# Cell work of each expert moved by a gate unit, a second place for the forget gate, and halves stored in pairs, in a language-model tower on one core

## The chip, the core and the metric

One NeuronCore of a Trainium2 chip runs the whole program as one launch. The metric is device time in microseconds, from the first to the last instruction and what the launch adds around it, as the median of three executions.

## What is computed

16 sequences of 512 tokens go through one block. Tokens become 128 features: an embedding and a projected spectrum per frame. Then h = h + attention(layernorm(h)), with 8 heads of 16, 64 summary tokens of full attention and a window of 17 for the other 448. Then comes the part that takes most of the time, a mixture of 8 recurrent experts, of which each token is given 2:

```python
logits = flat_x @ router_w + router_b
top_vals, top_idx = jax.lax.top_k(logits, K)          # K = 2 of E = 8
rw = jax.nn.softmax(top_vals, axis=1)
mask = (top_idx.T[:, None, :] == jnp.arange(E)[None, :, None])
expert_x = (mask[..., None] * flat_x[None, None]).reshape(K, E, S_, B_, I_)
def step(carry, xt):                                   # scanned over the 16 sequences
    h, c = carry
    i_, f_, g_, o_ = jnp.split(xt @ Wi + h @ Wh + b, 4, axis=-1)
    c = sigmoid(f_) * c + sigmoid(i_) * tanh(g_)
    h = sigmoid(o_) * tanh(c)
    return ((h, c), h @ Wo + bo)
y = jnp.einsum('ken,nk,keno->no', mask, rw, out)
```

Every expert sees every token of both choices, masked to zero where it was not chosen, since its state runs on.

## The kernel before

**Steps and units.** A step of the recurrence is one sequence. It has 32 gate units t = 4e + g: expert e = 0 to 7, and within it the gates I, G, F, O (g = 0 to 3). Each engine has a loop over s and t, written out by hand, and works through its list in order; nothing is planned by a scheduler. Beside the units of step s every engine runs `front(t, s + 1)`, the piece of embedding, attention and routing of the next sequence that the tables `PE_AT`, `ACT_AT`, `DVE_AT` and `SP_AT` (lines 56 to 63) give to unit t. Unit t of TensorE, ScalarE and VectorE are the same t, each after what the engine waits for.

**A gate.** TensorE (`unit_gate`, line 486) makes a gate of both choices, 128 x 1024, in 12 matmuls of 512 columns (line 506): weights and moving data are split into a high and a low 16-bit half, and three of the four products are taken, for input and state. There are two gate banks, so gate n waits for the tanh of gate n-2. ScalarE (`gate_tanh`, line 644) takes the tanh into a place of `tmp` (sigmoids are tanhs of half the argument).

**The cell on VectorE**, per expert, each operation on 128 x 1024: `input_part` (line 1000, writes (1+I)G), `cell` (line 1010: (1+F)C, line 1013, then C, line 1017), ScalarE's `cell_tanh` (line 658), which writes into F's only place, `hidden` (line 987: h in O's place), ScalarE's `split_hi` (line 664: high half of h), `hidden_lo` (line 995: low half), and `chosen` (line 1020): a predicated copy takes h of the choice that the token made, a product with its weight (line 1032) goes to `z32`. TensorE multiplies that by Wo (`unit_y`, line 509) into one bank; after all experts `y_out`, `y_back` and `add_y` bring it to the output. `masked_input` (line 975) makes the masked input of the next expert.

**Order on VectorE before** (lines 1044 to 1067). g=0: hidden(e-1), front. g=1: masked_input(e+1), hidden_lo(e-1), front, input_part(e). g=2: chosen(e-1), front, cell(e). g=3: front. In unit 30 masked_input of the next step's expert 0 comes first.

**SyncE** has the queue of DMA issues, in order too (lines 359 to 373). In units g=1 it loads masks for expert e+2 (`mask_in`, line 330). In units g=3 it loads the two row broadcasts of expert e+1 (`rows_in`, line 341), after waiting for the product of chosen(e-1):

```python
                if n >= 2:
                    sp.wait_ge(s_z, n - 1)
```

In unit 28 it stores the next step's masks and weights to DRAM (`SP_AT["rows"]`, line 312); in units 29 and 30 it broadcasts the masks of experts 0 and 1 back, after both stores have landed; in unit 31 come the rows of expert 0, and in unit 0 the next token ids (`sp_ids`, line 319), which line 779 turns into a one-hot and line 420 into the embedding.

**The routing** ends on VectorE with the front of unit 26 (line 973, the router weights); TensorE transposes them in unit 27 (line 483), and ScalarE evicts them (lines 639 and 642).

**Attention's block-diagonal weights.** `diag` holds, for 28 blocks of 16 queries, the heads of q and later the windows of v in a block-diagonal form, as two planes of 16-bit halves. It is filled by four DMAs from `pr` (SyncE, unit 6, line 310) and again from `vwin` (ScalarE's queue, unit 9, line 619) and read as 128-column weights, 84 times by line 447 and 84 times by line 459. The windows of v are made by two transposes, one a plane (line 824).

## Time and profile before

| | us |
|---|---|
| median of three executions | 1915.93 (1915.46 to 1918.11) |
| the profiled execution | 1918.11 |
| its span | 1916.3 |
| TensorE busy, matmul | 1729.1 (90%) |
| VectorE busy | 1559.5 (81%) |
| ScalarE busy | 991.9 (52%) |
| first gate matmul | at 120.2 |
| span of one steady step | about 114 |

Busy is the time in which an engine had an instruction under way, as a share of the span. Matmuls overlap in the pipeline and their ends are modelled, so TensorE's share is not a share of its peak. The granted clock of TensorE is 0.97 of full over the span, 1.00 in most of the steady part. A number in brackets behind a timeline row is the idle time of the engine before it, with what ended it. All times of views are from the start of the span.

### The profile page before, as it was taken

The page shows a single profiled execution, that of the slowest core. Times are in us where ns is not written, and L with a number is a line of the kernel's source. Part 1 is how long each engine was busy: PE and PEld are TensorE (multiplying, and loading weights), DVE is VectorE, ACT ScalarE, POOL GpSimd, SP SyncE. Part 2 cuts the span into 40 slices and gives each one's busy share as a digit, 9 for nine tenths or more (in the row PEclk, how much of TensorE's full clock was granted, in tenths as well). Part 3 has the DMA queues.
Part 4 walks back from the last instruction along what each step waited for, and adds up shares of the span by engine and source line. Part 5 has one row for each costly group of instructions (what it writes and reads, how often), then busy time and mean ns, then how long its engine had stood idle before and what let it go on. Part 6 is the DMA issues. An engine that isn't in the chain of part 4 may idle for free.

```text
span 1916.3 us, 25885 instructions
## 1 busy us (share of the span) xinstructions
PE 1729.1 (90%) x9898; PEld 837.6 (44%) x9898; DVE 1559.5 (81%) x2433; ACT 991.9 (52%) x1114; POOL 65.2 (3%) x42
## 2 busy tenths in 40 slices
PE   3457799999999999999999999999999999999998
PEld 2223344444444444444444444444444444444443
DVE  2649698897988889798898988889898888979865
ACT  3234554646555555645545455455555555564544
POOL 1000000000000000000000000000000000000000
PEclk9668899999999999999999999999999999999999
DMA  3113241413314132232313224151331413223221
GB/s 114 20 41 74 57 67 46 77 37 67 63 49 74 39 70 52 52 70 51 67 45 69 51 57 67 44 80 37 63 66 46 76 37 71 53 50 67 55 61 36
DMA packets 318594, 110.95 MB, mean 58 GB/s; under 512 B 240331, under 2 KB 299581, under 8 KB 318471
## 3 DMA queue, kind: packets, MB, share of 16 engines
q1 hardware_dynamic: 202758, 101.96, 23.9%
q10 hardware_dynamic: 115712, 7.34, 3.8%
q8 instruction: 78, 1.28, 0.3%
q14 instruction: 46, 0.37, 0.1%
HBM read 89.84 MB, written 4.74 MB: 49 GB/s over the span
## 4 chain that ended last, share of the span: by engine, by line
PE 40%; DVE 33%; DMA 8%; issue 7%; ACT 5%; ACTq 4%; SPq 1%; POOL 0%; DVEq 0%
PE gates L506 25%; ACTq L619 4%; DVE C L1017 4%; DVE tmp L1007 4%; DMA masks<-mask_scratch 3%; DVE tmp L1013 3%; DMA prod<-in_x_ids 3%; DVE xm L985 3%; PE yp L512 3%; DVE Hs L997 3%; DVE tmp L1028 3%; DVE xn L795 2%; PE FA L447 2%; ACT tmp L655 2%; PE FA L459 2%
## 5 line engine op out<-in xcount | busy, mean ns | idle before, releaser
L655 ACT ACTIVATE tmp<-gates,bias_sb 128x1024 f32<-128x1024 f32 x504 | 557.5, 1109 | 558.6 <-PE gates L506 496.1
L506 PE MATMUL gates<-xm,wi_sb 128*128 128x512 f16 x3024 | 747.3, 384 | 46.2 <-ACT tmp L655 31.0
L506 PE MATMUL gates<-Hs,wh_sb 128*128 128x512 f16 x2880 | 704.4, 381 | 0.0
L506 PEld LDWEIGHTS gates<-xm,wi_sb 128*128 128x128 f16 x3024 | 290.3, 99 | 435.3 <-issue 105.1
L506 PEld LDWEIGHTS gates<-Hs,wh_sb 128*128 128x128 f16 x2880 | 283.2, 98 | 344.3 <-issue 8.0
L662 ACT ACTIVATE tmp<-C 128x1024 f32<-128x1024 f32 x128 | 135.2, 1057 | 226.4 <-DVE C L1017 223.2
L992 DVE SCALAR_TENSOR_TENSOR tmp<-tmp 128x1024 f32<-128x1024 f32 x128 | 155.9, 1218 | 71.8 <-ACT tmp L662 71.8
L1007 DVE SCALAR_TENSOR_TENSOR tmp<-tmp 128x1024 f32<-128x1024 f32 x120 | 144.9, 1208 | 46.4 <-ACT tmp L655 44.9
L985 DVE TENSOR_TENSOR xm<-xs,masks 128x2048 f16<-128x2048 f16 x128 | 155.2, 1212 | 32.7 <-DMA masks<-mask_scratch 32.7
L997 DVE SCALAR_TENSOR_TENSOR Hs<-tmp,Hs 128x1024 f16<-128x1024 f32 x120 | 146.4, 1220 | 37.7 <-ACT Hs L666 36.7
L1013 DVE SCALAR_TENSOR_TENSOR tmp<-tmp,C 128x1024 f32<-128x1024 f32 x120 | 146.4, 1220 | 14.4 <-ACT tmp L655 14.0
L1017 DVE SCALAR_TENSOR_TENSOR C<-tmp 128x1024 f32<-128x1024 f32 x120 | 147.0, 1225 | 4.1
L666 ACT ACTIVATE Hs<-tmp 128x1024 f16<-128x1024 f32 x120 | 126.5, 1055 | 31.2 <-DVE tmp L992 30.7
L512 PE MATMUL yp<-z,wo_sb 128*128 128x512 f32 x256 | 134.9, 609 | 8.2 <-DVE z L1032 8.2
L1105 POOL TENSOR_TENSOR rstd<-veps,mhalf 128x4 f32<-128x4 f32 x32 | 61.6, 1926 | 1682.6 <-DVE veps L922 1114.8
L1032 DVE TENSOR_TENSOR z<-tmp,roww 128x512 f32<-128x512 f32 x128 | 88.6, 692 | 13.6 <-DVE tmp L1028 0.5
L1028 DVE COPY_PREDICATED tmp<-rowk,tmp 128x512 f32<-128x512 uint16 x128 | 93.0, 727 | 0.1
L512 PEld LDWEIGHTS yp<-z,wo_sb 128*128 128x128 f32 x256 | 48.0, 194 | 38.8 <-issue 12.2
L459 PE MATMUL FA<-vwin,diag 128*128 128x32 f16 x1344 | 36.3, 177 | 7.4 <-DVE vwin L882 7.4
L447 PEld LDWEIGHTS FA<-xn,diag 128*128 128x128 f16 x1344 | 38.2, 97 | 8.1 <-issue 5.5
L459 PEld LDWEIGHTS FA<-vwin,diag 128*128 128x128 f16 x1344 | 36.0, 96 | 12.5 <-DVE vwin L882 9.2
L447 PE MATMUL FA<-xn,diag 128*128 128x32 f16 x1344 | 39.1, 178 | 0.0
(155 smaller groups left out, 1218.9 us busy)
## 6 DMA issues: line engine op xcount, KB each, us to landing
masks<-mask_scratch SPq DMA_DIRECT2D x128, 256.0 KB, 5.0
roww<-mw_scratch SPq DMA_DIRECT2D x128, 256.0 KB, 4.0
rowk<-mask_scratch SPq DMA_DIRECT2D x128, 128.0 KB, 3.0
diag<-pr SPq DMA_DIRECT2D x64, 112.0 KB, 4.3
diag<-vwin ACTq DMA_DIRECT2D x64, 112.0 KB, 4.8
out_dram<-h SPq DMA_DIRECT2D x16, 256.0 KB, 3.7
C<-in_wi SPq DMA_DIRECT2D x1, 2048.0 KB, 10.9
C<-in_wh SPq DMA_DIRECT2D x1, 2048.0 KB, 15.6
```

Source lines behind the costliest of these rows:

```text
L506: last = mm(gates[:, slot, k * SEQ:(k + 1) * SEQ], w, v, start=(i < K), stop=(i >= len(seq) - K))
L512: mm(yp[:, :], wo_sb[:, e, :], z32[:, :], start=False, stop=(e == E - 1)).then_inc(s_y, 1)
L655: A(tmp[:, gate_at(gate, e), :], gates[:, (n - 1) % 2, :], ACT.Tanh, bias=bias_sb[:, e, gate:gate + 1], scale=UNSCALE).then_inc(s_tanh, 1)
L662: A(tmp[:, TANH_C, :], C[:, e, :], ACT.Tanh, scale=0.5).then_inc(s_tc, 1)
L666: A(Hs[:, e, HI, :], tmp[:, gate_at(O, e), :], ACT.Copy, scale=V_SCALE).then_inc(s_hhi, 1)
L985: TT(xm[:, e % 2, :, :, :], xv, mv_, ALU.mult).then_inc(s_xm, 1)
L992: STT(out=at, in0=at, scalar=1.0, in1=tmp[:, TANH_C, :], op0=ALU.add, op1=ALU.mult).then_inc(s_h, 1)
L997: STT(out=Hs[:, e, LO, :], in0=tmp[:, gate_at(O, e), :], scalar=V_SCALE, in1=Hs[:, e, HI, :], op0=ALU.mult, op1=ALU.subtract).then_inc(s_h ...
L1007: STT(out=at_i, in0=at_i, scalar=1.0, in1=at_g, op0=ALU.add, op1=ALU.mult).then_inc(s_u, 1)
L1013: STT(out=at_f, in0=at_f, scalar=1.0, in1=C[:, e, :], op0=ALU.add, op1=ALU.mult).then_inc(s_v, 1)
L1017: STT(out=C[:, e, :], in0=at_f, scalar=0.5, in1=tmp[:, gate_at(I, e), :], op0=ALU.mult, op1=ALU.add).then_inc(s_c, 1)
L1028: V.copy_predicated(at[:, 0:SEQ], rowk1[:, e % 2, :].bitcast(u16), at[:, SEQ:2 * SEQ]).then_inc(s_sel, 1)
```

## The change

The cell of expert e moves behind its O gate: VectorE's order becomes g=0: cell(e-1), front; g=1: masked_input(e+1), front, hidden(e-1); g=2: front, input_part(e); g=3: hidden_lo(e-1), chosen(e-1), front. ScalarE takes the cell tanh after the next expert's I tanh and the high half in g=2. TensorE's y matmuls and the bias of y move from g=0 to g=1, SyncE's store from unit 9 to 10. `tmp` has eight places: F has two, and the cell tanh goes to its own expert's F place. The weighted state stays in the upper half of O's place, so `z32` and the wait on it go, and O's tanh waits for the y matmul of two experts back. In `qz`, the v halves, `vwin` and `diag` the two 16-bit halves of a number lie side by side, so that one 32-bit transpose and 32-bit DMA elements carry both, and the matmuls of lines 447 and 459 read their weights at a stride of two. The waits and order of `rows_in`, `mask_in` and the stores on SyncE are as before.

```diff
@@ -85,14 +85,13 @@
         Hs = sb("Hs", [P, E, 2, K * SEQ], f16)
-        tmp = sb("tmp", [P, 7, K * SEQ])
+        tmp = sb("tmp", [P, 8, K * SEQ])
...
         roww = sb("roww", [P, 2, SEQ])
-        z32 = sb("z32", [P, SEQ])
@@ -116,7 +115,7 @@
         oW = sb("oW", [P, NW])
-        diag = sb("diag", [P, 2, NBLK, NG, 2 * DH], f16)
+        diag = sb("diag", [P, NBLK, NG, 2 * DH])
@@ -131,12 +130,13 @@
         wT = rows[WT0:WT0 + E, :]
-        qz = pr[:, :].bitcast(f16).rearrange("p (v j c q) -> p v j c q", v=2, j=NBLK, c=2)
+        qz = pr[:, :].bitcast(f16).rearrange("p (j c q v) -> p j c q v", j=NBLK, c=2, v=2)
...
         pr16, prT16 = pair16(pr[:, :], NBLK * KB), pair16(prT[:, :], NBLK * KB)
-        vw16 = vwin[:, :].bitcast(f16).rearrange("p (v j d) -> p v j d", v=2, j=NBLK)
-        vhl = ew[:, 0:TF + 2 * PAD].bitcast(f16).rearrange("p (v t) -> p v t", v=2)
+        vwj = vwin[:, :].rearrange("p (j d) -> p j d", j=NBLK)
+        vp = ew[:, 0:TF + 2 * PAD]
+        vp16 = pair16(vp, TF + 2 * PAD)
@@ -170,15 +170,18 @@
         def gate_at(gate, e):
 
-            return {I: e % 2, G: 2 + e % 2, F: 4, O: 5 + e % 2}[gate]
-
-        TANH_C = gate_at(F, 0)
+            return {I: 0, G: 2, F: 4, O: 6}[gate] + e % 2
+
+        def chosen_at(e):
+
+            return tmp[:, gate_at(O, e), SEQ:2 * SEQ]
...
         fid = tmp[0:NFFT, 2, 512:512 + NBJ].bitcast(i32)
-        diag_flat = diag[:, :, :, :, :].rearrange("p v j g d -> p (v j g d)")
-        onehot64 = diag_flat[0:NFFT, 2 * VOCAB * NBJ:3 * VOCAB * NBJ]
-        mag = diag_flat.bitcast(f32)[0:NFREQ, 0:VOCAB * NBJ]
+        diag_flat = diag[:, :, :, :].rearrange("p j g d -> p (j g d)")
+        diag16 = diag_flat.bitcast(f16).rearrange("p (j m v) -> p j m v", j=NBLK, v=2)
+        onehot64 = diag_flat.bitcast(f16)[0:NFFT, 2 * VOCAB * NBJ:3 * VOCAB * NBJ]
+        mag = diag_flat[0:NFREQ, 0:VOCAB * NBJ]
@@ -307,8 +310,8 @@
                     for g in range(NG):
-                        load(diag[32 * g:32 * g + 32, :, :, g, :].rearrange("p v j d -> p (v j) d"),
-                             qz[32 * g:32 * g + 32, :, :, :, :].rearrange("p v j c q -> p (v j) (c q)"), S["qbd"])
+                        load(diag[32 * g:32 * g + 32, :, g, :],
+                             pr[32 * g:32 * g + 32, :].rearrange("p (j d) -> p j d", j=NBLK), S["qbd"])
@@ -359,7 +362,7 @@
             def step(s, par, first, last):
...
                     e, g = t // NG, t % NG
-                    if t == 9 and not first:
+                    if t == 10 and not first:
@@ -444,7 +447,7 @@
                             for qv, kv in ((HI, HI), (HI, LO), (LO, HI)):
-                                last = mm(FA[:, r, jj * KB:(jj + 1) * KB], diag[:, qv, j, :, :].rearrange("p g d -> p (g d)"),
+                                last = mm(FA[:, r, jj * KB:(jj + 1) * KB], diag16[:, j, :, qv],
@@ -456,7 +459,7 @@
                         for vv, pv in ((HI, HI), (HI, LO), (LO, HI)):
-                            last = mm(FA[:, j // HB, (j % HB) * KB:(j % HB + 1) * KB], diag[:, vv, j, :, :].rearrange("p g d -> p (g d)"),
+                            last = mm(FA[:, j // HB, (j % HB) * KB:(j % HB + 1) * KB], diag16[:, j, :, vv],
@@ -509,7 +512,7 @@
             def unit_y(s, e):
...
                 pe.wait_ge(s_z, s * E + e + 1)
-                mm(yp[:, :], wo_sb[:, e, :], z32[:, :], start=False, stop=(e == E - 1)).then_inc(s_y, 1)
+                mm(yp[:, :], wo_sb[:, e, :], chosen_at(e), start=False, stop=(e == E - 1)).then_inc(s_y, 1)
@@ -530,11 +533,11 @@
                         unit_gate(s, e, g, first)
-                    if g == 0 and e == 2:
+                    if g == 1 and e == 2:
                         y_bias(s)
-                    if g == 0 and e >= 2:
+                    if g == 1 and e >= 2:
                         unit_y(s, e - 2)
-                    elif g == 0 and not first:
+                    elif g == 1 and not first:
@@ -590,7 +593,7 @@
                     for c in range(2):
-                        last = A(qz[:, HI, :, c, :], qT[:, NW:SEQ].rearrange("p (j q) -> p j q", q=QB), ACT.Copy,
+                        last = A(qz[:, :, c, :, HI], qT[:, NW:SEQ].rearrange("p (j q) -> p j q", q=QB), ACT.Copy,
@@ -605,7 +608,7 @@
                     act.wait_ge(S["v"], b1)
-                    A(vhl[:, HI, :], vf[:, :], ACT.Copy, scale=Q_SCALE).then_inc(S["vhi"], 1)
+                    A(vp16[:, :, HI], vf[:, :], ACT.Copy, scale=Q_SCALE).then_inc(S["vhi"], 1)
@@ -616,8 +619,7 @@
                     for g in range(NG):
-                        act.dma_start(diag[32 * g:32 * g + 32, :, :, g, :].rearrange("p v j d -> p (v j) d"),
-                                      vw16[32 * g:32 * g + 32, :, :, :].rearrange("p v j d -> p (v j) d")) \
+                        act.dma_start(diag[32 * g:32 * g + 32, :, g, :], vwj[32 * g:32 * g + 32, :, :]) \
@@ -646,10 +648,10 @@
                 m = s * E + e
-                if gate == F and m >= 1:
-                    act.wait_ge(s_h, m)
+                if gate == F and m >= 2:
+                    act.wait_ge(s_h, m - 1)
                 elif gate == O and m >= 2:
-                    act.wait_ge(s_z, m - 1)
+                    act.wait_ge(s_y, m - 1)
@@ -657,9 +659,9 @@
             def cell_tanh(s, e):
                 act.wait_ge(s_c, s * E + e + 1)
-                if s == 0 and e:
-                    act.wait_ge(s_h, e)
-                A(tmp[:, TANH_C, :], C[:, e, :], ACT.Tanh, scale=0.5).then_inc(s_tc, 1)
+                if s == 0 and e >= 2:
+                    act.wait_ge(s_h, e - 1)
+                A(tmp[:, gate_at(F, e), :], C[:, e, :], ACT.Tanh, scale=0.5).then_inc(s_tc, 1)
@@ -676,12 +678,14 @@
                         y_out(s - 1)
-                    if g == 0 and e and not last:
+                    if g == 0 and e:
+                        cell_tanh(s, e - 1)
+                    elif g == 0 and not first:
+                        cell_tanh(s - 1, E - 1)
+                    if g == 2 and e and not last:
                         split_hi(s, e - 1)
-                    elif g == 0 and not e and not first:
+                    elif g == 2 and not e and not first:
                         split_hi(s - 1, E - 1)
-                    if g == 3:
-                        cell_tanh(s, e)
@@ -712,6 +716,7 @@
             run_steps(step_p)
+            cell_tanh(STEPS - 1, E - 1)
@@ -803,26 +808,23 @@
                     for c in range(2):
-                        last = STT(out=qz[:, LO, :, c, :], in0=qT[:, NW:SEQ].rearrange("p (j q) -> p j q", q=QB),
-                                   scalar=parq[:, c:c + 1], in1=qz[:, HI, :, c, :], op0=ALU.mult, op1=ALU.subtract)
+                        last = STT(out=qz[:, :, c, :, LO], in0=qT[:, NW:SEQ].rearrange("p (j q) -> p j q", q=QB),
+                                   scalar=parq[:, c:c + 1], in1=qz[:, :, c, :, HI], op0=ALU.mult, op1=ALU.subtract)
...
                     wait("vhi", b1)
-                    STT(out=vhl[:, LO, :], in0=vf[:, :], scalar=Q_SCALE, in1=vhl[:, HI, :],
+                    STT(out=vp16[:, :, LO], in0=vf[:, :], scalar=Q_SCALE, in1=vp16[:, :, HI],
...
 
-                    for v in (HI, LO):
-                        own = vhl[:, v, :]
-                        win = bass.AP(tensor=own.tensor, offset=own.offset, ap=[list(own.ap[0]), [QB, NBLK], [1, KB]])
-                        last = V.transpose(vw16[:, v, :, :], win)
-                    last.then_inc(S["vwin"], 1)
+                    win = bass.AP(tensor=vp.tensor, offset=vp.offset, ap=[list(vp.ap[0]), [QB, NBLK], [1, KB]])
+                    V.transpose(vwj, win).then_inc(S["vwin"], 1)
@@ -989,7 +991,7 @@
                 at = tmp[:, gate_at(O, e), :]
-                STT(out=at, in0=at, scalar=1.0, in1=tmp[:, TANH_C, :],
+                STT(out=at, in0=at, scalar=1.0, in1=tmp[:, gate_at(F, e), :],
@@ -1026,10 +1028,8 @@
                 V.copy_predicated(at[:, 0:SEQ], rowk1[:, e % 2, :].bitcast(u16), at[:, SEQ:2 * SEQ]).then_inc(s_sel, 1)
-                if n:
-                    dve.wait_ge(s_y, n)
                 dve.wait_ge(s_sel, n + 1)
-                TT(z32[:, :], at[:, 0:SEQ], roww[:, e % 2, :], ALU.mult).then_inc(s_z, 1)
+                TT(chosen_at(e), at[:, 0:SEQ], roww[:, e % 2, :], ALU.mult).then_inc(s_z, 1)
@@ -1041,30 +1041,32 @@
 
-                    if g == 0 and e:
-                        hidden(s, e - 1)
-                    elif g == 0 and not first:
-                        hidden(s - 1, E - 1)
+                    if g == 0 and e and not first:
+                        cell(s, e - 1)
+                    elif g == 0 and s >= 2 and not e:
+                        cell(s - 1, E - 1)
...
                         masked_input(s, e + 1, par, first and e == 0)
-                    if g == 1 and e and not last:
-                        hidden_lo(s, e - 1)
-                    elif g == 1 and not e and not first:
-                        hidden_lo(s - 1, E - 1)
...
                         masked_input(s + 1, 0, 1 - par, False)
-                    if g == 2 and e:
+                    if g == 3 and e and not last:
+                        hidden_lo(s, e - 1)
+                    elif g == 3 and not e and not first:
+                        hidden_lo(s - 1, E - 1)
+                    if g == 3 and e:
                         chosen(s, e - 1)
-                    elif g == 2 and not first:
+                    elif g == 3 and not first:
...
                         front(t, s + 1, 1 - par)
-                    if g == 1:
+                    if g == 1 and e:
+                        hidden(s, e - 1)
+                    elif g == 1 and not first:
+                        hidden(s - 1, E - 1)
+                    if g == 2:
                         input_part(s, e, first)
-                    if g == 2 and not first:
-                        cell(s, e)
@@ -1079,6 +1081,7 @@
             run_steps(step)
+            cell(STEPS - 1, E - 1)
@@ -1095,7 +1098,7 @@
             pool.wait_ge(s_enc, 1)
-            G_.memset(diag_flat.bitcast(f32), 0.0).then_inc(s_zero, 1)
+            G_.memset(diag_flat, 0.0).then_inc(s_zero, 1)
```

## Rows read from the trace of the kernel before

**Rows 1.** Busy time of one step: stretch, length, then each engine's busy us (count).
```profile
1116.70:1230.30 113.60, 109.47 (x630) 53.06 (x630) 98.04 (x154) 60.91 (x70) 3.82 (x2) 0.98 0.29 58
```

**Rows 2.** Waits of the whole run: who waited for whom, us, times, longest.
```profile
ACT tmp L662 <- DVE C L1017: 223.2, 110, 3.2
...
DVE tmp L992 <- ACT tmp L662: 71.8, 65, 1.1
```

**Rows 3.** Timeline of one step, all engines: start us, us, what [idle before].
```profile
1114.95 0.69 DVE L1032 TENSOR_TENSOR z<-tmp,roww 128x512 f32<-128x512 f32 x1
...
1116.55 0.18 DVE L973 TENSOR_TENSOR pr<-pr 128x32 f32<-128x32 f32 x1
...
1122.79 0.90 SPq L338 DMA_DIRECT2D masks<-mask_scratch  x2
...
1127.23 1.23 DVE L985 TENSOR_TENSOR xm<-xs,masks 128x2048 f16<-128x2048 f16 x1 [1.37 <-DMA masks<-mask_scratch]
...
1129.21 0.69 DVE L1032 TENSOR_TENSOR z<-tmp,roww 128x512 f32<-128x512 f32 x1
...
1131.21 0.34 SPq L284 DMA_DIRECT2D prod<-in_x_ids  x1
...
1134.90 0.47 DVE L779 TENSOR_SCALAR rows<-prod,vcol 16x512 f32<-16x512 int32 x1 [0.26 <-DMA prod<-in_x_ids]
...
1135.43 1.16 PE L420 MATMUL FB<-table,rows 41*128 41x128 f32 x8 [0.67 <-DVE rows L779]
...
1143.80 1.22 DVE L1017 SCALAR_TENSOR_TENSOR C<-tmp 128x1024 f32<-128x1024 f32 x1
...
1148.44 0.69 ACT L588 ACTIVATE qT<-FA,bqkv_sb 128x512 f32<-128x512 f32 x1
...
1151.21 0.28 DVE L801 TENSOR_TENSOR prod<-qT,kw 128x64 f32<-128x64 f32 x1 [1.40 <-ACT kf L598]
...
1169.52 1.22 DVE L1007 SCALAR_TENSOR_TENSOR tmp<-tmp 128x1024 f32<-128x1024 f32 x1 [1.77 <-ACT tmp L655]
1170.35 2.66 ACTq L619 DMA_DIRECT2D diag<-vwin  x2
...
1174.27 1.22 DVE L1013 SCALAR_TENSOR_TENSOR tmp<-tmp,C 128x1024 f32<-128x1024 f32 x1 [1.08 <-ACT tmp L655]
...
1230.19 0.18 DVE L973 TENSOR_TENSOR pr<-pr 128x32 f32<-128x32 f32 x1
```

**Rows 4.** Groups of instructions by form: xcount | busy, mean ns.
```profile
L1105 POOL TENSOR_TENSOR rstd<-veps,mhalf 128x4 f32<-128x4 f32 x32 | 61.6, 1926 | 1682.6 <-DVE veps L922 1114.8 <-DVE veps L789 567.7
...
L824 DVE STREAM_TRANSPOSE vwin<-ew 128x896 f16<-128x896 f16 x32 | 33.6, 1087 | 0.1
...
L624 ACT ACTIVATE pr<-vwin 128x896 f16<-128x896 f32 x16 | 19.0, 1187 | 5.4 <-DVE vwin L875 5.4
...
L882 DVE STREAM_TRANSPOSE vwin<-pr 128x896 f32<-128x896 f32 x16 | 17.8, 1112 | 0.6
...
L614 ACT ACTIVATE pr<-pr 128x896 f32<-128x896 f32 x16 | 15.0, 937 | 10.6 <-issue 10.6
```

**Rows 5.** Timeline of TensorE in the startup and in step 0.
```profile
70.36 0.55 PE L441 MATMUL FA<-bandb,identb 128*128 128x448 bf16 x1 [7.32 <-DMA diag<-pr]
...
198.18 0.95 PE L477 MATMUL FA<-rw_sb,xnT 128*128 128x8 f32 x8
```

**Rows 6.** Chain of waits: start us, us, what; startup, then a steady step.
```profile
39.33 1.67 DMA prod<-in_x_ids
...
111.80 1.43 DMA mw_scratch<-rows
...
1149.50 5.18 PE gates L506 x24
...
1163.45 1.05 PE FA L447 x42
```

**Rows 7.** DMA issues of the page: KB each, median us from issue to landing.
```profile
roww<-mw_scratch SPq DMA_DIRECT2D x128, 256.0 KB, 4.0
```

## The prediction

> **What bounds the kernel now.** I read first the busy time over one whole step, from the router weights of one step to those of the next [rows 1]: VectorE is busy 98.0 of 113.6 us and TensorE 109.5. TensorE's figure flatters it, because matmul ends are modelled. It still idles 4.1 us, so it is near its floor, and neither engine alone sets the period. Then the waits [rows 2]: ScalarE stands 223 us of the run before the tanh of the cell, waiting for C, and VectorE in turn 72 us for that tanh, 1.1 each time. Last, the timeline [rows 3], because the period must be closed by something that returns once a step. It is a loop. Let w be the end of line 973, the router weights (1116.73). The weights become masks in DRAM, the masks are broadcast back (issue 1122.79, used 1127.23), VectorE masks the next input and makes chosen(6) (its product starts at 1129.21 and takes 0.69), SyncE then issues the row loads and behind them the next ids (1131.21), line 779 starts at 1134.90 and TensorE's embedding at 1135.43. So w to embedding is 18.7 us; embedding to the next w (1230.37) is 94.9 us, nearly all VectorE work; together 113.6. In the first part VectorE and TensorE have slack, in the second they have little. The question is what the change does to either part.
>
> **Startup and layout.** (a) Pairs of halves: two 16-bit transposes of 1087 ns become one 32-bit of about 1112 ns [rows 4]. Handed over a tenth earlier, this saves VectorE 1.0 us a step. (b) The four loads into diag, twice a step, carry the same bytes in half as many runs of double length. The last two of ScalarE's four issues hold it for 2.66 us [rows 3]; nothing shows the shorter form, so its bounds are unchanged and half. I take half, because the later issues of the four are the slow ones, as if they waited for room for their runs; nothing behind them is then late. (c) Strided 16-bit writes: ScalarE took 1187 ns for 896 elements against 937 written whole [rows 4], so about 0.12 for each of three writes of some 450; bound 0 to 0.4 together, I take 0.25 before the keys. VectorE: 0.15 (0 to 0.3, from the same pair). (d) In the first front nothing covers the loads: TensorE stands 7.32 us for the first of them [rows 5]. Half saves some 3.6 (0 to 4). The second gives 1.4, then other VectorE work binds (0 to 1.4). Startup: -4.7, bounds 0 and -6. Step 0 has half of the gates and idles on every engine, so less coupling helps there; I estimate -4 (0 to -8).
>
> **Weights read at a stride of two.** 168 loads a step. At present a contiguous 128-column load and its 32-column matmul take 1.05 us for 42, 25 ns a pair [rows 6]; a pair with 32-bit weights, the other end, 0.95 for 8, some 112 ns with the overlap off [rows 5]. So the price is between 0 and 168 x 87 = 14.6 us a step. The moving side (prT) is already read at this stride inside such 25 ns pairs, which is the nearest row, so I take 0. The Trainium skill, "TensorE: Matmul & The Clock Gate", section "Weight-path perf modes", says two things: the fast load takes a "packed or strided" pattern, and it gains by reading 32 bits at a time, two bf16. By the second, a 32-bit read here would hold one wanted half and the gain would be gone. No row of this trace decides between them.
>
> **The cell order.** Per expert, VectorE goes from hidden(e-1), masked, hidden_lo(e-1), input part(e), chosen(e-1), cell(e) to cell(e-1), masked, hidden(e-1), input part(e), hidden_lo(e-1), chosen(e-1). A front stage now has less cell work ahead of it, by 1.2 to 3.9 us. ScalarE's tanh of the next gate no longer stands behind the cell tanh that waits for C. The doubled F place and the wait of O's tanh on the y matmul cost nothing: y(e-2) is issued after gate 1 of the expert, O's tanh follows gate 3. The wait of the product on y goes; it cost under 0.1 us each time. The y matmuls, the bias of y and the store move a unit later, with their inputs, and none of them was late.
>
> Now the loop, step by step, with steady durations (an operation hands over after 1.1 to 1.2 us, chosen after 1.5, a cell after 2.4).
>
> *w to embedding.* Before, chosen(5) was ahead of the weights: its product ended at 1115.64 [rows 3], and SyncE's row loads were out before w. Now input part(6), hidden_lo(5) and chosen(5) come behind the weights: 1.1 + 1.1 + 1.5 = 3.7. SyncE is in order, and its wait for this product stands ahead of the mask stores. So rowk and roww go out until w+4.2, the stores at w+4.6 and 5.0. ScalarE's mask rows, 2 us earlier than before since no cell tanh is ahead of them, gain nothing. The stores also stand in the queue behind the row broadcasts, 256 KB for roww alone [rows 7]. A load of ids alone landed in 1.67 us [rows 6]; right behind the row loads it takes 3.7 [rows 3]. So a small transfer lands only with the roww ahead of it, which takes 4.0 [rows 7]: w+8.2, stores w+8.6 (alone they took 1.43 [rows 6], which would be w+6.4). The broadcast takes 4.4: masked input at w+13.0 (before w+10.5). Then masked, input part(7), hidden_lo(6), chosen(6): 4.9, against 2.7 before; w+17.9. Row issues 1.3, ids 3.7, onehot 0.5: embedding at w+23.4. That is +4.7.
>
> *Embedding to next w.* Out: the same three operations now behind w, -3.7. In: hidden(7), +1.1. Transpose and strides -0.85. VectorE's idle today: two waits of 1.1 for a cell tanh [rows 2], 1.40 at line 801, 1.77 and 1.08 for gate tanhs [rows 3]; 6.5 in all. The waits for tanhs go: the masked input lies between a cell and its hidden state, and the gate tanhs are read a unit later. But ScalarE now has the cell tanh of expert 0 ahead of the q, k and v evictions of unit 4, and it waits for cell(0). Today that cell ends at 1145.02, 9.6 us after the embedding [rows 3]. hidden(7) now comes before it, +1.1. So do two new gaps, both estimates: 0.9 before the moments, where hidden_lo(7) covered the eviction of h, and 1.0 before the norm, since GpSimd's root takes 1.9 [rows 4] and only hidden(7) lies beside it. So cell(0) ends at +12.6 and q starts at +13.6, where it was +13.0; 0.25 more for the strides, and the 2.8 from q to line 801 as today: +16.6, where VectorE, now without hidden(0) and hidden_lo(0) ahead of that line, has arrived at +13.6. It waits 3.0, not 1.4. One more gap of 2.2 opens at unit 11, where hidden_lo needs the high half that ScalarE makes only after unit 10's tanh, and some 0.3 at the projection. The new idle time is 0.9 + 1.0 + 3.0 + 2.2 + 0.3 = 7.4, against 6.5: +0.9. Sum -3.7 + 1.1 - 0.85 + 0.9 = -2.5 (bounds: -6 with the new gaps halved, -1 with diag issues as slow as today, 1.3 more).
>
> *Period:* +4.7 - 2.5 = +2.2 us, 115.8. TensorE, walked the same way, is ready for the mask transposes just as the weights are, so it gives nothing more to gain. Fourteen periods: +31. Into the last step the masks alone are late: +2. The tail is unchanged.
>
> **Sum.** -4.7 - 4 + 31 + 2 = +24. The profiled execution took 1918.1 (span 1916.3); the median of the three is 1915.9, 2.2 lower. I put the difference on the median: 1940. A measurement of this kernel can tell some 0.2% (3.8 us) from no change.
>
> **Rivals.**
> 1. *The mask stores do not wait behind the row loads.* Then the masks land 2.1 us earlier, the period is 113.7, and only startup and step 0 remain: about 1907, faster. Against it stands the ids load, 1.67 alone and 3.7 behind the rows. It decides from 2 us less than I take in the first part. Chance 0.15.
> 2. *TensorE's stalls go.* If the fronts, 1.2 to 3.9 us earlier, hide the loop (say the ids wait falls within work), the 4.1 us idle of TensorE go: 14 x -4.1 - 9 = -66, about 1850. For it: ScalarE's 223 us before the cell tanh. Against it: the loop goes through SyncE and two broadcasts, which no reordering shortens. Chance 0.13.
> 3. *The strided weight load is slow.* A matmul column takes 0.42 ns (216 ns for 512: 24 gate matmuls in 5.18 us [rows 6]), so a load of 128 columns one by one is 54 ns. That is 29 more a pair: 168 x 29 = 4.9 a step, with 16 fronts +78, little of it covered since both windows stand between the engines: about 2010. It decides from some 10 ns more a pair. This is what the sentence on 32-bit reads would give. Chance 0.12.
> 4. *It cancels.* The two parts of the period err by 1 us each, so that +2.2 is +0.6 or less: 1912 to 1920, in effect a change that does not do what it says. Chance 0.10.
>
> **Chances and range.** My forecast has 0.50, with a range of its own of 1922 to 1962 (1.3 us a step either way). Slower by over 0.2%: 0.50 and 0.12, less a margin at the lower edge: 0.60. Same: 0.13. Faster: rivals 1 and 2, 0.27 beyond the margin. The range 1898 to 1975 takes in rival 1 and leaves out rivals 2 and 3 for the most part.
>
> **What would show it.** Right: from the end of line 973 to line 420's embedding some 23 us instead of 18.7; the last roww issued behind w and the mask stores waiting for it, with the masked input some 13 us after w; line 801's wait at 3 us; the tanh of C no longer the largest wait of ScalarE; the period near 115.8. The transposes must be 16 of about 1.1 us, the diag packets half. Wrong: mask broadcasts issued at w+6.5; the two groups of 42 pairs longer than 1.05 us; or a period under 113, with TensorE's gates back to back across units 0, 3 and 17.

## The result and the profile after

The changed kernel took 1969.87 us, median of four executions (1965.93 to 1978.42), against 1917.02 (1915.46 to 1919.09) for the kernel before: a ratio of 1.0281, 95% interval 1.0242 to 1.032, so 53 us slower. The profiled execution took 1966.9, its span is 1965.1; 48.8 more than the span before, and that difference is what the sums below are held against. The forecast was +24. Longer executions of the changed kernel have a lower mean granted clock: 1965.93 us at 0.947, 1966.90 at 0.946, 1972.83 at 0.943, 1978.42 at 0.939.

The chain that ended last, in the w to embedding part of step 12 (w = 1493.28 is the end of the router weights, now line 975): start us, us, what.

```profile
1495.65 0.75 DVE tmp L1030
...
1496.42 0.70 DVE tmp L1032
...
1497.14 0.32 SPq L351
...
1497.50 0.43 SPq L353
...
1498.04 0.37 SPq L287
...
1498.46 3.46 DMA mw_scratch<-rows
...
1501.93 4.45 DMA masks<-mask_scratch
...
1506.41 1.23 DVE xm L987
...
1512.52 3.84 DMA prod<-in_x_ids
...
1516.91 1.17 PE FB L423 x8
```

This is the loop of [rows 3] with the new order in it. SyncE waits for chosen(5), whose product ends at w+3.8, issues rowk and roww, and only then the two stores (w+4.8 and w+5.2). The store of 16 KB takes 3.46 us, with roww ahead of it; in [rows 6] it took 1.43. The mask broadcasts go at w+8.65 (forecast w+8.6), the masked input starts at w+13.1 (w+13.0), the embedding at w+23.6 (w+23.4). In the kernel before, the stores went at w+4.0 and w+4.6 and the mask broadcasts at w+6.05. So of the 2.6 us by which the broadcasts come later, 2.0 are the longer landing and 0.6 the later issue.

The timeline of VectorE and ScalarE's queue in the same step, all on rows that the forecast named: start us, us, what, idle before.

```profile
1516.38 0.48 DVE L784 TENSOR_SCALAR rows<-prod,vcol 16x512 f32<-16x512 int32 x1 [2.52 <-DMA prod<-in_x_ids]
...
1522.26 1.11 DVE L800 TENSOR_SCALAR xn<-h_sb,mv,rstd 128x128 f32<-128x128 f32 x4 [0.90 <-POOL rstd L1108]
...
1533.49 0.27 DVE L806 TENSOR_TENSOR prod<-qT,kw 128x64 f32<-128x64 f32 x1 [2.75 <-ACT kf L601]
...
1548.88 2.23 ACTq L622 DMA_DIRECT2D diag<-vwin  x2
...
1554.26 1.23 DVE L999 SCALAR_TENSOR_TENSOR Hs<-tmp,Hs 128x1024 f16<-128x1024 f32 x1 [2.03 <-ACT Hs L668]
...
1595.42 1.11 DVE L800 TENSOR_SCALAR xn<-h,mv,rstd 128x128 f32<-128x128 f32 x4 [0.90 <-POOL rstd L1108]
```

Line 806 starts 16.6 us after the embedding, as forecast, after 2.75 us of waiting (3.0 forecast, [rows 3] 1.40). The gaps of 0.90 and 2.03 are there too (1.0 and 2.2). The last row is one the forecast missed: the second norm waits for GpSimd's root as the first does.

The window view shows what the forecast did not have. The two parts of step 12 and of step 13: stretch, length, then each engine's busy us (count) for PE, PEld, DVE, ACT and POOL, then the granted clock, the DMA share and GB/s.

```profile
1493.30:1516.90 23.60, 18.81 (x85) 8.41 (x83) 15.06 (x16) 12.16 (x13) 0.00 (x0) 1.00 0.29 68
1516.90:1609.40 92.50, 89.96 (x550) 44.55 (x550) 82.20 (x137) 50.27 (x58) 3.84 (x2) 1.00 0.26 54
1609.40:1633.30 23.90, 19.73 (x80) 8.53 (x80) 15.01 (x16) 11.60 (x12) 0.00 (x0) 0.93 0.28 68
1633.30:1728.50 95.20, 93.41 (x547) 45.85 (x548) 82.44 (x137) 49.77 (x57) 3.85 (x2) 0.95 0.25 52
```

Step 12 ran at full clock throughout its second part and took 92.5 us from embedding to next w, where the forecast had 94.9 - 2.5 = 92.4. Step 13, with the same VectorE work (82.2 and 82.4), had a granted clock of 0.95 and took 95.2. The same in the timeline of TensorE at the end of step 13's first part:

```profile
1619.80 1.46 PE L509 MATMUL gates<-Hs,wh_sb 128*128 128x512 f16 x6
1623.80 1.64 PE L509 MATMUL gates<-xm,wi_sb 128*128 128x512 f16 x6 [2.55 <-issue]
1625.24 2.77 PE L509 MATMUL gates<-Hs,wh_sb 128*128 128x512 f16 x6
1627.80 1.74 PE L509 MATMUL gates<-xm,wi_sb 128*128 128x512 f16 x6
...
1633.33 1.16 PE L423 MATMUL FB<-table,rows 41*128 41x128 f32 x8 [1.64 <-DVE rows L784]
1634.42 2.04 PE L509 MATMUL gates<-xm,wi_sb 128*128 128x512 f16 x6
1636.25 2.62 PE L509 MATMUL gates<-Hs,wh_sb 128*128 128x512 f16 x6
```

Six gate matmuls take 1.46 us; after a wait of 2.55 us for the masked input some take 2.77, and again after the wait for the onehot. The second part of step 10, cut at such a stretch (same columns as above):

```profile
1287.00:1344.90 57.90, 56.14 (x389) 27.69 (x388) 51.20 (x63) 34.59 (x40) 0.22 (x1) 1.00 0.35 67
1344.90:1348.40 3.50, 3.50 (x19) 1.32 (x16) 3.43 (x7) 1.06 (x1) 0.00 (x0) 0.52 0.02 7
1348.40:1358.70 10.30, 10.30 (x48) 5.56 (x47) 7.52 (x11) 4.29 (x4) 0.00 (x0) 1.00 0.22 64
```

For 3.4 us the granted clock is half, 1.2 GHz instead of 2.4, and then whole again. From the first gate of step 1 to the tail, where TensorE runs out of work, the record of the clock has 33 such pieces, and 5 in the kernel before. The mean granted clock fell from 0.970 to 0.946. From here on a *halved stretch* is one of these pieces. Except at +75, they begin near the end of a TensorE wait of 1 to 3 us, from 0.7 us before it to 2.3 behind it. In the second part their places are +1 to +2 us behind the start of the embedding (wait for the onehot), about +62 (wait of 1.76 for the values' transpose), and about +75, where no wait over 0.3 us stands near. Not every wait is followed by one: the wait of 1.76 us for the values is there in each of steps 1 to 14, a halved stretch at +62 in six of them.

That wait is new. In steps 1 to 14 of the kernel before TensorE never waits for the values' transpose. The wait comes with the cell order, not with the queue: it is there at 1.76 us when the queue is mended (the first run of section 1), and not when the old order gets the queue loss (its reverse) or the layout (section 2).

What a stretch at +62 does is seen where VectorE next needs TensorE, at the projection, in step 12 (none) and in step 13 (one):

```profile
1591.16 0.69 DVE L914 TENSOR_TENSOR h<-FB,h_sb 128x512 f32<-128x512 f32 x1 [0.89 <-PE FB L469]
...
1710.06 0.69 DVE L914 TENSOR_TENSOR h<-FB,h_sb 128x512 f32<-128x512 f32 x1 [2.57 <-PE FB L469]
```

In all six steps with a stretch at +62 this wait is 2.10 to 2.57 us, in steps 1 to 14 without one 0.89 to 0.99 (before 0.90 to 0.94).

Other rows. The waits of the whole run, who waited for whom, us in all, times, longest, and then groups by form:

```profile
ACT tmp L664 <- DVE C L1019: 227.7, 113, 4.3
...
DVE xm L987 <- DMA masks<-mask_scratch: 84.3, 16, 9.2
...
DVE tmp L994 <- ACT tmp L664: 34.2, 22, 3.6
```

```profile
L827 DVE STREAM_TRANSPOSE vwin<-ew 128x896 f32<-128x896 f32 x16 | 17.7, 1104 | 0.0
```

```profile
1542.55 1.05 PE FA L450 x42
```

The tanh of C waits as long as before (223.2 in [rows 2]), and it is still ScalarE's largest wait for another engine's operand; the forecast's sign "no longer the largest wait" was wrong, and a run below shows what that wait does. The transposes are 16 of 1.1 us. The 42 pairs with weights read at a stride of two take 1.05 us in the chain, as in [rows 6]: 25 ns a pair, so rival 3 is false. The packets of ScalarE's queue fell from 115712 to 58368, and a load into diag lands in 3.2 us instead of 4.8.

### The profile page after: what moved, and what is told of

The parts are those of the page before. It is cut to its first block, busy times and chain, and to the rows that moved or that the text cites. A ratio compares the mean times of both kernels' runs of the same rounds, so it can differ in the third digit from the quotient of the medians.

```text
span 1965.1 us, 25741 instructions
## 1 busy us (share of the span) xinstructions
PE 1767.7 (90%) x9898; PEld 853.8 (43%) x9898; DVE 1547.6 (79%) x2417; ACT 994.5 (51%) x1114; POOL 64.6 (3%) x42
## 3 DMA queue, kind: packets, MB, share of 16 engines
q10 hardware_dynamic: 58368, 7.34, 2.6%
## 4 chain that ended last, share of the span: by engine, by line
PE 39%; DVE 36%; DMA 10%; issue 7%; ACT 3%; POOL 2%; SPq 2%; ACTq 0%; DVEq 0%
PE gates L509 25%; DVE Hs L999 5%; DMA masks<-mask_scratch 4%; DVE tmp L1009 3%; DVE tmp L1030 3%; DVE tmp L1015 3%; DMA prod<-in_x_ids 3%; DVE xm L987 3%; DMA mw_scratch<-rows 3%; PE yp L515 2%; POOL rstd L1108 2%; DVE tmp L1032 2%; DVE tmp L994 2%; PE FA L462 2%; PE FA L450 2%
## 5 line engine op out<-in xcount | busy, mean ns | idle before, releaser
L509 PE MATMUL gates<-xm,wi_sb 128*128 128x512 f16 x3024 | 775.9, 395 | 52.3 <-issue 25.0
L509 PE MATMUL gates<-Hs,wh_sb 128*128 128x512 f16 x2880 | 724.3, 389 | 0.0
L509 PEld LDWEIGHTS gates<-xm,wi_sb 128*128 128x128 f16 x3024 | 297.9, 101 | 455.1 <-issue 155.0
L509 PEld LDWEIGHTS gates<-Hs,wh_sb 128*128 128x128 f16 x2880 | 289.3, 100 | 364.3 <-issue 43.4
L664 ACT ACTIVATE tmp<-C 128x1024 f32<-128x1024 f32 x128 | 135.2, 1056 | 227.7 <-DVE C L1019 227.7
L515 PE MATMUL yp<-tmp,wo_sb 128*128 128x512 f32 x256 | 135.1, 610 | 5.9 <-DVE tmp L1032 5.8
L1032 DVE TENSOR_TENSOR tmp<-tmp,roww 128x512 f32<-128x512 f32 x128 | 88.6, 692 | 4.4
L515 PEld LDWEIGHTS yp<-tmp,wo_sb 128*128 128x128 f32 x256 | 47.6, 193 | 36.8 <-issue 12.4
L784 DVE TENSOR_SCALAR rows<-prod,vcol 16x512 f32<-16x512 int32 x16 | 7.6, 474 | 55.6 <-DMA prod<-in_x_ids 55.6
L423 PE MATMUL FB<-table,rows 41*128 41x128 f32 x128 | 19.8, 298 | 29.7 <-DVE rows L784 29.7
```

The lines of the kernel that those rows point to most:

```text
L509: last = mm(gates[:, slot, k * SEQ:(k + 1) * SEQ], w, v, start=(i < K), stop=(i >= len(seq) - K))
L515: mm(yp[:, :], wo_sb[:, e, :], chosen_at(e), start=False, stop=(e == E - 1)).then_inc(s_y, 1)
L664: A(tmp[:, gate_at(F, e), :], C[:, e, :], ACT.Tanh, scale=0.5).then_inc(s_tc, 1)
L1032: TT(chosen_at(e), at[:, 0:SEQ], roww[:, e % 2, :], ALU.mult).then_inc(s_z, 1)
```

## The experiments

The kernels ran in three groups, each on one chip with its own runs of the kernel before (medians 1914.21, 1918.91 and 1918.84). Ratios are against those. The parts of a step, means over steps 2 to 13, worked out from the timelines (us):

```
kernel                                 w to masks  w to embedding  embedding to next w  period
before                                   6.05        19.04           94.88              113.9
after                                    8.61        23.95           93.79              117.7
rows behind the masks                    4.04        19.98           93.31              113.3
ids early                                8.63        22.33           93.41              115.8
rows behind the masks, ids early         4.59        18.56           94.05              112.6
two waits filled                         8.68        23.87           93.26              117.1
before, rows behind w                    8.93        22.55           94.67              117.2
before, layout alone                     6.05        19.29           93.78              113.1
before, layout and ids early             6.05        18.73           93.82              112.5
stores on ScalarE's queue                4.83        20.69           94.06              114.8
three waits filled                       8.77        24.17           92.80              117.0
```

("w to masks" ends at the issue of the mask broadcasts. Each row is one profiled execution; that of "rows behind the masks" took 1904.88 us, 4.4 less than the median of that kernel.)

### 1. Where SyncE issues the rows

The changed kernel, the row broadcasts of expert 7 behind the mask broadcasts:

```diff
+                    if t == 30:
+                        rows_in(s, E - 1)
-                    if g == 3 and e < E - 1:
+                    if g == 3 and e < E - 2:
                         rows_in(s, e + 1)
-                    elif g == 3 and not last:
+                    elif g == 3 and e == E - 1 and not last:
```

> The changed kernel, with SyncE's two row loads of expert 7 issued after the mask stores and broadcasts (unit 30) instead of before them (unit 27). Theory Q (the mask stores wait on SyncE and in the queue behind row loads that now wait for chosen(5)): from the end of the router weights to the masked input 9 us instead of 13.1, to the embedding 19.6 instead of 23.6, so 14 periods of 4 us less, 1969.9 - 56 = some 1914, and less still if TensorE's clock falls less often. Rival R (it is VectorE's and ScalarE's order that costs: the q and k evictions behind the cell tanh, the later hidden_lo): the masks come earlier, but VectorE and ScalarE need as long from the embedding on and the period falls by 1 us or less, to 1955 or more.

Measured: 1909.3 (1904.65 to 1915.49, ten executions), ratio 0.9976 (0.9964 to 0.9989). Its timeline, step 12 (w = 1445.92):

```profile
1447.31 0.32 SPq L287 DMA_DIRECT2D mask_scratch<-ew  x1
1447.92 0.28 SPq L287 DMA_DIRECT2D mw_scratch<-rows  x1
1449.37 0.90 SPq L341 DMA_DIRECT2D masks<-mask_scratch  x2
1450.32 0.46 SPq L351 DMA_DIRECT2D rowk<-mask_scratch  x1
```

The stores go at w+1.4 and w+2.0 and the broadcasts 1.45 us after the second. Moving the two row loads, and the wait for chosen(5) with them, takes 60 us out of the run (56 expected).

The reverse, in the kernel before: its cell order and layout stay, only the rows of expert 7 are issued behind the wait for the mask rows and ahead of the stores.

```diff
+                    if t == 28:
+                        if not last:
+                            sp.wait_ge(S["mrow"], s + 2)
+                        rows_in(s, E - 1)
                     if not last:
                         front(t, s + 1)
...
-                    if g == 3 and e < E - 1:
+                    if g == 3 and e < E - 2:
                         rows_in(s, e + 1)
-                    elif g == 3 and not last:
+                    elif g == 3 and e == E - 1 and not last:
```

> The kernel before with its cell order and layout unchanged; only SyncE's two row broadcasts of expert 7 are issued behind its wait for the mask rows and ahead of the mask stores, where the new cell order puts them. Before, the stores go at w+4.0 and w+4.6 and the mask broadcasts at w+6.1. Theory Q (the queue is the whole loss): rows at w+4.0, stores at w+4.9 and land only with roww at w+8.4, mask broadcasts at w+8.7, masked input at w+13.1, embedding later by 2.6 us a step; period 113.8 + 2.6 = 116.4, 15 periods: 1914 + 39 = 1953. Theory C on top (each longer TensorE wait also costs clock): another 0.5 to 1.7 us a step, 1960 to 1975, and the granted clock below that of before with a halved stretch behind the masked input's wait. Rival (the new cell order itself costs, the queue alone little): under 1925.

Measured: 1968.23 (1967.7 to 1971.89), ratio 1.0258 (1.0242 to 1.0273). The timeline, w = 1376.52:

```profile
1380.97 0.43 SPq L350 DMA_DIRECT2D roww<-mw_scratch  x1
1381.50 0.37 SPq L284 DMA_DIRECT2D mask_scratch<-ew  x1
1381.92 0.32 SPq L284 DMA_DIRECT2D mw_scratch<-rows  x1
1385.61 0.90 SPq L338 DMA_DIRECT2D masks<-mask_scratch  x2
```

The position of two DMA issues alone, without any cell moved, costs nearly what the whole change costs (1953 was expected of the queue alone, 1960 to 1975 with the clock). w to embedding is 3.5 us longer, 2.9 of it at the mask broadcasts (2.6 expected) and 0.5 at the embedding, for which TensorE itself is late here. Embedding to next w is as before (94.67). The only halved stretches in it begin at +75, where they cost nothing in the changed kernel either; the others begin 6 to 8 us ahead of the embedding, and in steps 2 to 13 w to embedding is 22.8 us with one and 22.1 without. So this run doesn't show what a stretch at +1 or +62 would cost under the old order.

The third question is whether the small store is late because of the queue or because of the engines that all queues share. In the changed kernel ScalarE issues both stores on its own queue, and SyncE no longer does:

```diff
                     A(wT, FB[WT0:WT0 + E, :], ACT.Copy).then_inc(S["wT"], 1)
+                    act.wait_ge(S["mrow"], b1)
+                    act.wait_ge(s_enc_out, 32)
+                    act.dma_start(mask_dram[bass.ds(b, 1), :, :].rearrange("a r t -> (a r) t"), mrow[:, :]) \
+                        .then_inc(S["mout"], 16)
+                    act.wait_ge(S["wT"], b1)
+                    act.dma_start(mw_dram[b, :, :], wT).then_inc(S["mout"], 16)
```

> The changed kernel with one edit: the mask and weight stores are issued by ScalarE on its own queue right after it has evicted both, and no longer by SyncE behind its wait for chosen(5) and behind the two row broadcasts. ScalarE has the mask rows at w+2.6 and the weights at w+3.2, so the stores go at about w+3.3 and w+3.8, at the same time as the row broadcasts on SyncE's queue (w+3.9 and w+4.2). Theory Q (a small store lands late because it stands behind a broadcast in one queue): the stores land in 1.4 us, the mask broadcasts go at about w+5.4 instead of w+8.6; they share the engines with the rows, so 0 to 1 us of that is given back: 2.2 to 3.2 us a step, 1970 less 35 to 48, 1922 to 1935. Rival (the transfers of both queues share the same engines, and the stores wait for roww there too): mask broadcasts still at w+8.2 to w+8.6, 1960 to 1970.

Measured: 1926.32 (1922.19 to 1928.45), ratio 1.0036 (1.0025 to 1.0048). The timeline, w = 1464.23:

```profile
1466.23 0.96 ACTq L646 DMA_DIRECT2D mw_scratch<-rows  x1
1468.09 0.32 SPq L347 DMA_DIRECT2D rowk<-mask_scratch  x1
1468.45 0.43 SPq L349 DMA_DIRECT2D roww<-mw_scratch  x1
1469.05 0.88 SPq L337 DMA_DIRECT2D masks<-mask_scratch  x2
1474.40 1.22 DVE L989 TENSOR_TENSOR xm<-xs,masks 128x2048 f16<-128x2048 f16 x1 [1.60 <-DMA masks<-mask_scratch]
```

The broadcasts go at w+4.8 instead of w+8.6, right after SyncE has issued roww, so the stores had landed by then, at most 2.8 us after the second was issued, with the row broadcasts under way. 0.4 us a step comes back as a slower mask broadcast (here 5.35 us to its use). The stores here were issued 2 us ahead of the rows, and no longer behind the wait for chosen(5), so this shows that a store issued ahead of the rows escapes the loss; whether a store issued at the same moment as the rows on another queue would also be quick, it does not show.

### 2. The layout alone

The kernel before with diag, qz and the halves of v in pairs (all edits of the diff that touch them), and nothing else.

```diff
-        diag = sb("diag", [P, 2, NBLK, NG, 2 * DH], f16)
+        diag = sb("diag", [P, NBLK, NG, 2 * DH])
...
-                    for v in (HI, LO):
...
+                    V.transpose(vwj, win).then_inc(S["vwin"], 1)
```

> The kernel before with the storage in pairs of halves alone: one 32-bit transpose in place of two, diag filled in runs of double length, weights read at a stride of two; cell order, places of tmp and SyncE's order as before. By the forecast's own terms: startup -4.7, VectorE -0.85 a step, most of which counts between the embedding and the next w, and the four diag issues of ScalarE shorter by 1.3: 1914 - 5 - 15 x 0.85 = 1896 (1890 to 1909). Rival (strided weights or strided writes cost): 1914 or more. Rival (the clock moves instead): anywhere within 10 us of it, with another count of halved stretches.

Measured: 1897.8 (1895.03 to 1899.61), ratio 0.9885 (0.9871 to 0.99). Embedding to next w is 1.1 us shorter (forecast 0.85), and the first onehot of the loop is made 3.5 us earlier. This half of the change does what it should.

If the parts multiply, which no run shows, the queue is 1.0258, the layout 0.9885, and what is left for the cell order is 1.0281 / (1.0258 x 0.9885) = 1.014. With the queue mended it is 0.9976 / 0.9885 = 1.009. By this the order loses about 1%; a closer pair of runs, in section 3, puts it at 0.3%.

### 3. The ids, and the repaired queue

```diff
-                    if not last:
+                    if not last and t != SP_AT["ids"]:
                         front(t, s + 1)
+                    if t == 24 and s + 2 < STEPS:
+                        sp_ids(s + 2)
...
+            sp_ids(1)
```

> The changed kernel, with the token ids of the step after next loaded in unit 24 instead of behind the row loads that wait for chosen(6). Theory Q: the onehot no longer waits (2.5 us of VectorE each step), so the embedding comes 20.9 us after the router weights instead of 23.6, the masked input still 13.1 after them; 14 x -2.6 = -36, some 1934. Rival R: TensorE's embedding comes earlier but the evictions of q and k still wait for cell(0), whose place behind the norm is unchanged; if that is what holds the period, it falls by under 1 us, 1956 or more.

Measured: 1943.09 (1938.52 to 1947.65), ratio 1.0151 (1.013 to 1.0172), 27 us of the 36 expected: the wait for the ids goes, and another is behind it (1.65 us from onehot to embedding instead of 0.53).

> Both edits of the two runs before. Theory Q: the two waits are in one loop, so the gains add up until TensorE's own work binds: embedding some 17.8 us after the router weights (TensorE is ready then), -4 and -1.8 a period, and the clock falls rarely: 1969.9 - 14 x 6 = some 1886. Rival R: at most 2 us a period together, 1940.

Both edits: 1893.28 (1890.09 to 1895.11), ratio 0.9889 (0.9874 to 0.9904), 1.1% below the kernel before, and 77 us of the 84 expected. Here each of steps 1 to 14 has a halved stretch at about +62, behind the 1.76 us for the values, and VectorE's wait at the projection is 1.9 to 2.5 us in all of them.

The same ids edit on the kernel before with the layout:

> The kernel before with its own cell order, the layout in pairs of halves (1897.8 alone) and the ids of each sequence loaded a step early. It is the fair partner of the repaired new order: if the new cell order is worth something once its queue loss is mended, this stays above 1869. The ids wait goes (3.8 us from the ids issue to the onehot), but chosen(6)'s product then has nothing behind it and TensorE and VectorE take over: with the new order the same edit gave 16 us in the presence of the row repair (1909.3 to 1893.3). Expected 1897.8 less 5 to 20: 1885. Rival (nothing behind the ids but TensorE's own work, already near its floor of 109.5 busy of 113): 1893 to 1898.

Measured: 1891.95 (1891.1 to 1892.73), ratio 0.986 (0.9845 to 0.9875), only 6 us below the layout alone. There the ids were nearly hidden. Both this kernel and the one before it have the layout, early ids and mask stores that no row load holds up, since the rows go out ahead of w in this one and behind the mask broadcasts in the other. Otherwise they differ in the cell order alone: 0.986 with the old one, 0.9889 (0.9874 to 0.9904) with the new. So once its queue loss is mended, the new order as it stands costs 0.3%, little more than these runs can tell from nothing.

### 4. TensorE's clock

The changed kernel with matmuls that nobody reads in place of waits, in units 0 and 1:

```diff
+            def keep_busy(s, n):
+                pe.wait_ge(S["wT"], s + 1)
+                for _ in range(n):
+                    mm(FB[:, :], wi_sb[:, 0, HI, 0:P], wi_sb[:, 0, HI, 0:SEQ], start=True, stop=True)
...
+                    if t == 0 and not first:
+                        keep_busy(s, 8)
...
+                    if t == 1 and not first and not last:
+                        keep_busy(s, 8)
```

> The changed kernel, with 8 idle matmuls of 512 columns (1.7 us, into a bank that is free then) ahead of TensorE's two long waits of a step, the one for the masked input in unit 0 and the one for the onehot in unit 1. Nothing else waits less. Theory C (TensorE's clock falls to half, 1.2 GHz, for 3.4 or 6.8 us after these gaps, about twice a step, and that is what lies between the 115.8 us of a step without such a stretch and the mean of 117.5): the halved stretches go mostly, mean granted clock from 0.946 to 0.965 or more, time falls by 20 to 30 us although 16 x 3.4 us of matmuls were added. Rival D (the clock falls for another reason, with no link to these gaps): clock as before, time unchanged or longer by up to 50 us.

Measured: 1960.06 (1958.87 to 1963.9), ratio 1.0243 (1.0228 to 1.0258). It gained 10 us, half of the lower figure expected. The halved stretches fell from 33 to 15, and the mean granted clock rose from 0.946 to 0.963 (0.965 expected).

Then a third filler, ahead of the values:

```diff
                 if t == PE_AT["values"]:
+                    if not is_zero(b):
+                        pe.wait_ge(S["pn"], b1)
+                        for _ in range(8):
+                            mm(FA[:, 0, :], wi_sb[:, 0, HI, 0:P], wi_sb[:, 0, HI, 0:SEQ], start=True, stop=True)
                     pe.wait_ge(S["prT"], b1)
```

> The changed kernel with 8 idle matmuls of 512 columns at three of TensorE's waits: before unit 0 and in unit 1, as in the run before with two filled gaps (1960.06), and now also ahead of the values product in unit 18, where it waits 1.76 us each step. They take the place of a wait and release nothing. Theory C (a wait of about 1.8 us there brings a stretch of halved clock at +62 and often another at +75 us behind the embedding, and the two together cost up to 2.4 us of embedding to next w): these stretches go, embedding to w is 92.4 to 92.7 in every step instead of 93.3 on average, so 14 x 0.8 = 11 us less than with two gaps filled: 1949. Rival (the halved stretches follow the load in another way, or cost nothing because VectorE sets the time): 1956 to 1964. Rival (the fillers run over the wait and cost 0.5 to 1.7 a step): 1967 or more.

Measured: 1958.38 (1956.3 to 1959.02), ratio 1.0203 (1.0186 to 1.022). By the ratio that is 0.4% (8 us) below two fillers, by the profiled spans nothing (1957.1 and 1957.2); 11 us were expected, so the number was wrong. The place was right: no stretch begins at +62 in any of steps 1 to 13, where the changed kernel has six and two fillers left four. Embedding to next w fell by 0.46 us a step, and the wait at the projection is 0.88 to 0.94 us in each of steps 1 to 14. But four stretches at the embedding and four at +74 remain, and w to embedding grew by 0.3.

The steps of these three kernels, sorted by where halved stretches begin, give the price, since the work of a step is the same:

```
embedding to next w, us, by the halved stretches of that part
  none, or only at +74 to +77      92.4 to 92.7    (changed, two filled, three filled)
  at +1 to +2 alone                93.2 to 93.4
  at +62 (and +75)                 93.9 to 94.0
  at +1 to +2, +62 (and +75)       94.4 to 95.1
```

A stretch at +75, in VectorE's busiest part, is free. One at +1 or +62 costs 0.8 and 1.4 us. On average over steps 2 to 13 the changed kernel pays 93.8 - 92.5 = 1.3 us a step. With three fillers, which take away no other work, that part is 92.80: 1.0 of the 1.3 us is back.

The four executions of the changed kernel say the same. The slowest has 16.5 us more of clock lost than the fastest ((1 - 0.939) x 1976.6 against (1 - 0.947) x 1964.1), which is ten halved stretches more, and took 12.5 us longer: an estimate of some 1.3 us a stretch.

### 5. TensorE's wait for the values

The repaired kernel (rows behind the masks, ids early) with `values=19` in place of 18 in `PE_AT`:

> The changed kernel with rows behind the masks and ids early (1893.28, period 112.6), and TensorE's values product moved from unit 18 to unit 19, so that it no longer stands waiting 1.9 us for VectorE's transpose; its reader comes 4 us later on VectorE anyway. Theory C (a wait of TensorE of about 2 us costs itself and 1.7 us of halved clock behind it): the period falls by 1.9 + 1.7 to about 109.1, so 1893 - 15 x 3.5 = 1840, and one of the two halved stretches per step is gone. Rival (the wait alone counts): 1893 - 28 = 1865. Rival (VectorE or ScalarE closes the loop, and the wait turns up elsewhere): 1885 to 1893.

Measured: 1882.13 (1879.77 to 1886.77), ratio 0.9801 (0.9784 to 0.9817): a gain, but far from 1840. The wait moved, and the stretch with it: twelve of steps 1 to 14 have one at about +61, where VectorE then waits 2.55 to 2.87 us at the projection instead of 1.17. The timeline of that kernel:

```profile
1167.50 1.09 ACT L662 ACTIVATE tmp<-gates,bias_sb 128x1024 f32<-128x1024 f32 x1
...
1171.64 1.23 DVE L1024 SCALAR_TENSOR_TENSOR C<-tmp 128x1024 f32<-128x1024 f32 x1
...
1172.89 1.06 ACT L669 ACTIVATE tmp<-C 128x1024 f32<-128x1024 f32 x1 [4.30 <-DVE C L1024]
...
1174.32 2.10 ACT L662 ACTIVATE tmp<-gates,bias_sb 128x1024 f32<-128x1024 f32 x2
...
1175.47 2.07 PE L514 MATMUL gates<-xm,wi_sb 128*128 128x512 f16 x6 [2.05 <-ACT tmp L662]
```

ScalarE stands 4.30 us at the tanh of C with the next gate's tanh behind it, and TensorE waits 2.05 us for that gate's bank. This is the new order's own price, and the forecast said the opposite ("ScalarE's tanh of the next gate no longer stands behind the cell tanh that waits for C").

Two edits on ScalarE follow. First, the q, k and v evictions of unit 4 ahead of that unit's tanh of C:

```diff
+                    if t == ACT_AT["qkv"] and not last:
+                        front(t, s + 1)
                     if g == 0 and e:
                         cell_tanh(s, e - 1)
...
-                    if not last:
+                    if t != ACT_AT["qkv"] and not last:
                         front(t, s + 1)
```

> As the run with values in unit 19, and ScalarE evicts q, k and v in unit 4 ahead of the tanh of C of expert 0 instead of behind it. The forecast held that this tanh holds up the evictions and through them line 801 (now 806), which waits 2.9 us a step. If that wait is on the path: another -1.0 us a step, 15 us below the run with values in unit 19. If TensorE sets the period there (it idles 0.5 us at that place): within 4 us of it, while the wait at 806 falls from 2.9 to under 2.

Measured: 1869.04 (1868.88 to 1870.48), ratio 0.9738 (0.9724 to 0.9753), 13 us less (15 expected). VectorE's wait for the keys falls from 51.1 us in 16 times to 12.2 in 2. From step 6 on steps alternate: 92.1 us from embedding to next w without a halved stretch, 94.0 with one at +61.

Second, expert 3's tanh of C a unit later:

```diff
-                    if g == 0 and e:
+                    if (g == 0 and e and e != 4) or t == 17:
                         cell_tanh(s, e - 1)
-                    elif g == 0 and not first:
+                    elif t == 0 and not first:
                         cell_tanh(s - 1, E - 1)
```

> The fastest kernel so far (1869.04) with ScalarE's tanh of C of expert 3 moved from unit 16 to unit 17, behind that unit's gate tanh. In unit 16 to 17 ScalarE waits 4.3 us for C at this tanh, with the tanh of the next gate behind it, and TensorE then waits 2.05 us for the gate bank; in half of the steps a halved stretch follows and embedding to w is 94.0 instead of 92.15. If the order on ScalarE makes the TensorE wait: it goes, and with it the halved stretch; VectorE is busy throughout that part, so the 92.15 stays and the alternation goes: -0.9 us a step, 1856. If TensorE was setting the time there: up to -2.9 a step, 1828. Rival (hidden(3) on VectorE now waits for the tanh, 1 us): 1869 or more.

Measured: 1855.22 (1854.4 to 1858.7), ratio 0.9672 (0.9658 to 0.9686): 64 us below the kernel before, the fastest of all, and at the 1856 expected. Two steps of it in the window view, the part from embedding to next w, first with 3.4 us at half clock, then with 6.8:

```profile
1205.90:1297.10 91.20, 90.68 (x548) 44.79 (x548) 81.58 (x137) 50.70 (x58) 3.84 (x2) 0.98 0.30 59
...
1315.60:1408.30 92.70, 92.18 (x547) 45.27 (x547) 81.81 (x137) 50.56 (x58) 3.84 (x2) 0.96 0.30 57
```

TensorE now idles 0.5 us in the part. The stretches that remain begin at +71.5 to +73, 2 to 4 us behind the only wait over 0.3 us that is left near them, 0.44 us.

## Why the forecast was right or wrong

**Right: the direction, the loop and where it breaks.** SyncE's wait for chosen(5) ahead of the stores, the stores behind roww, w+8.6, w+13.0, w+23.4 were all within 0.3 us in step 12. As means w to embedding grew by 4.9 us (4.7 forecast). Experiment 1 and its reverse show that this is the cause of the loss: the queue position alone makes 1968 from the old kernel, and mending it takes 60 us from the new one. Rival 1, that the stores don't queue, is false by the chain's 3.46 us. Rival 3 is false by the 1.05 us row. Of the two things that the Trainium skill says in "TensorE: Matmul & The Clock Gate", section "Weight-path perf modes", this case's trace agrees with the first, a "packed or strided" pattern: 25 ns a pair at a stride of two is less than the 54 ns that 128 columns take one by one. The second, the gain of 32-bit reads, shows no loss here at a stride of two. Rival 4 is false by the total. Rival 2, that TensorE's stalls go, did not happen here; the last run reaches such a time (1855), but only with the queue, the ids, the values and two places on ScalarE changed as well.

**Wrong: the size, +48.8 in place of +24.** By the starts of the first gate of each step, the 14 periods gave +50.0 (forecast +31) and the ends -1.2 (forecast -6.7). So the miss is 19 in the periods and 5.5 at the ends.

*The periods.* The step that failed is "Embedding to next w: -2.5". It holds in the steps without a halved stretch at a place that counts (92.4 to 92.7 against a forecast 92.4) and fails in the others. Their mean with the others is 93.8: 1.3 us a step, 18 in all, of the 19. Another 0.2 a step, 3 in all, is in w to embedding (steps 2 to 13 stand for all fourteen here, so the two don't add up exactly). Two terms were left out. The first is the granted clock: the forecast knew that the queue would lengthen TensorE's waits in front of unit 0 and of the embedding, and gave these waits no price beyond themselves. The second is a wait. "TensorE, walked the same way, ... gives nothing more to gain" has no wait for the values' transpose, where TensorE now stands 1.76 us in every step; where no stretch follows it the part still has the forecast's length (92.4 to 92.7), but the stretches at +62 begin there, and they are the dearer ones. The kernel before had 5 halved stretches, four of them at +75, so the profile offered no row for the price. That the new order also took VectorE's cover away (busy 82.2 to 82.4 us of the part instead of 85.4) is likely but not shown: no run has a stretch at +1 or +62 under the old order.

Within the 92.5 smaller errors cancel: the second norm's 0.90 gap was not counted, against 0.25 too much at line 806, 0.3 at the projection, whose wait did not grow (0.89, before 0.92), 0.3 at two other gaps, and a layout worth 1.1 instead of 0.85. The upper bound for the strided weights was a little low: 0.95 us for 8 is 119 ns a pair, not 112, so 15.8 us a step instead of 14.6; measured was 0, so nothing hangs on it.

*The ends.* Startup was right: the first gate starts at 115.83 instead of 120.16, -4.3 for -4.7. Step 0 was not: +1.6 us where -4 was estimated. This is the second step that failed: the estimate ("idles on every engine, so less coupling helps there") priced the order only and left the queue loss out of step 0, although the same stores stand behind the same rows there. From the onehot made in step 0 to that made in step 1 it is 101.3 us before, 104.9 after, and 99.8 with the rows behind the masks. The last step was +1.6 for +2.

*A sign that was wrong.* The tanh of C stayed ScalarE's largest wait for another engine's operand (227.7 us). The forecast took the new place of that tanh, ahead of a gate tanh instead of behind one, as a gain. At the two places that were tried, units 4 and 16, where VectorE has a front stage ahead of the cell, it is a loss: moving the tanh or what stands behind it gave 13 us each.

**Open.** Why the clock halves is read here only by place: near waits of about 1 to 3 us, but not at each of them, and in many steps at +75 and +72, where the wait ahead is 0.44 us or none is seen. Fillers at three waits removed two thirds of the stretches and moved some. What the order itself loses (1% by division, 0.3% by the closer pair) was not traced place by place; the wait for the values and two waits on ScalarE are parts of it. The values and ScalarE edits were not tried with the old order, so that 1855 against 1892 does not say that the new order is the better one.

## What to carry to other kernels

When a step is moved past a wait, list every DMA that the same engine issues behind that wait and read what each of them waits for in its queue: two broadcasts ahead of one 16 KB store cost this kernel more than all of its other parts gained. In an in-order engine put the operation whose operand comes last behind those that are ready: twice on ScalarE this gave 13 us. And where a change lengthens TensorE's waits or makes a new one, price the clock too, from the steps of the trace that have a halved stretch and those that have none.

## What the runs showed of the hardware that was not expected

- A store of 16 KB issued right behind a 256 KB row broadcast in one queue lands 3.46 us later, with the broadcast; alone 1.43. Issued 2 us ahead of the broadcasts on another queue it had landed within 2.8.
- In the steady steps the granted clock halves for pieces of 3.41 us, seldom 6.83. A piece costs 0, 0.8 or 1.4 to 1.9 us according to its place: nothing at +75, 1.9 at +61, where VectorE then waits for TensorE at the projection (92.1 and 94.0 us in alternate steps of one kernel).
- The same wait of TensorE, 1.76 us for the values, went with a part of 92.4 to 92.7 us in the steps where no halved stretch followed it, and of 93.9 to 94.0 where one did at that place alone.
- 16-bit weights of 128 columns read at a stride of two load as fast as contiguous ones: 84 pairs of load and 32-column matmul in 2.1 us either way.
- Half as many descriptors of double length land in two thirds of the time (4.8 to 3.2 us), but the last two of ScalarE's four issues fell only from 2.66 to 2.23 us, not to half.
